# Quantised W1 rows of a four-layer residual kernel: turned through memory and VectorE instead of TensorE, and five of the seven threshold steps nested between VectorE and ScalarE

## The reference, cut to what matters

```
def _L1_cond_ref(x, weight, scale_log, codebook, lora_A, lora_B):
    lora_delta = lora_B @ lora_A * (32.0 / 64)
    cb = codebook / clip(max(abs(codebook)), 1e-08)          # 8 levels
    scale = exp(scale_log)                                    # one for each row and group of 128
    normalized = (weight + lora_delta).reshape(O, I // 128, 128) / scale
    thresholds = (cb[:-1] + cb[1:]) * 0.5                     # 7 thresholds
    idx = searchsorted(thresholds, normalized, side='left')
    quantized = cb[idx]
    w_q = quantized * scale
    return x @ (w_q + lora_delta).T

x = x + _L0_cond_ref(...)    # W0, with a low-rank part chosen by batch
x = x + _L1_cond_ref(...)    # W1, as above
x = x + _L2_cond_ref(...)    # W2, with a low-rank part chosen by batch
x = x + _L3_cond_ref(...)    # W3, with a router and eight small experts
```

## Time and profile before

| | |
|---|---|
| median of 3 runs (lowest to highest) | 594.34 us (594.05 to 594.41) |
| span of the profiled execution | 592.8 us |
| PE busy | 585.1 us, 99% |
| DVE busy | 447.3 us, 75% |
| ACT busy | 236.4 us, 40% |
| POOL busy | 111.9 us, 19% |
| granted TensorE clock | 1.000 |

### The profile page before, as it was taken

One profiled execution on the slowest core, in us unless ns is written; L12 is line 12 of the kernel. 1 busy time (PEld: TensorE's weight loads), 2 busy tenths in 40 slices (PEclk: granted clock), 3 DMA queues, 4 the chain that ended last, 5 costly groups with the idle time before them and its releaser, 6 DMA issues.

```text
span 592.8 us, 9183 instructions
## 1 busy us (share of the span) xinstructions
PE 585.1 (99%) x3152; PEld 522.2 (88%) x3152; DVE 447.3 (75%) x812; ACT 236.4 (40%) x482; POOL 111.9 (19%) x131
## 2 busy tenths in 40 slices
PE   7999999999999999999999999999999999999998
PEld 6999999899999999999787887787888888888887
DVE  4678998999989855897788999947474747474744
ACT  4534233445432216544465477323333333333331
POOL 3101010012000000336324011041212121212110
PEclk9999999999999999999999999999999999999999
DMA  8962230173000000000243000223031303131301
GB/s 258 231 173 79 87 110 2 26 187 125 1 2 1 1 0 2 2 0 2 25 87 77 1 1 1 65 79 105 37 101 41 107 34 102 40 94 48 107 1 71
DMA packets 56994, 37.19 MB, mean 63 GB/s; under 512 B 25924, under 2 KB 50756, under 8 KB 56964
## 3 DMA queue, kind: packets, MB, share of 16 engines
q1 hardware_dynamic: 56964, 36.79, 22.2%
HBM read 28.39 MB, written 8.39 MB: 62 GB/s over the span
## 4 chain that ended last, share of the span: by engine, by line
PE 73%; DVE 22%; issue 2%; ACT 1%; SPq 1%; DMA 1%; POOL 0%; DVEq 0%; ACTq 0%
PE acc L1864 39%; PE acc L1718 16%; DVE q L1244 6%; PE aux L1864 5%; DVE qtmp L1243 4%; PE acc L1985 4%; PE aux L1706 2%; PE acc L1987 2%; DVE hg_lo L1270 1%; PE acc L1993 1%; PE acc L1994 1%; DVE w_lo L1131 1%; DVE a_t L1255 1%; DMA g<-in_L_cond_W_dram 1%; DVE a_t L1246 1%
## 5 line engine op out<-in xcount | busy, mean ns | idle before, releaser
L1864 PE MATMUL acc<-b_hi,g_lo 128*128 128x512 f32 (+1 forms) x266 | 88.9, 389 | 0.1
L1864 PE MATMUL acc<-t_hi,g_lo 128*128 128x512 f32 x256 | 87.6, 400 | 0.0
L1718 PE MATMUL acc<-hg_hi,w_hi 128*128 128x352 f32 (+1 forms) x376 | 85.3, 334 | 1.6 <-DVE hg_lo L1270 0.8
L1718 PE MATMUL acc<-hg_lo,w_hi 128*128 128x352 f32 (+1 forms) x376 | 84.3, 331 | 0.0
L1718 PE MATMUL acc<-hg_hi,w_lo 128*128 128x352 f32 (+1 forms) x376 | 84.0, 330 | 0.0
L624 POOL TENSOR_TENSOR xr<-xr 128x512 f32<-128x512 f32 x32 | 41.1, 1308 | 144.3 <-DVE g_lo L1435 142.9
L1718 PEld LDWEIGHTS acc<-hg_hi,w_hi 128*128 128x128 f32 x376 | 65.1, 188 | 3.0 <-DVE hg_lo L1270 1.1
L1718 PEld LDWEIGHTS acc<-hg_hi,w_lo 128*128 128x128 f32 x376 | 65.8, 188 | 0.0
L1718 PEld LDWEIGHTS acc<-hg_lo,w_hi 128*128 128x128 f32 x376 | 65.8, 188 | 0.0
L1244 DVE TENSOR_TENSOR q<-q,qtmp 128x1024 f32<-128x1024 f32 x48 | 59.7, 1243 | 1.7
L1864 PEld LDWEIGHTS acc<-b_hi,g_lo 128*128 128x128 f32 x266 | 49.6, 188 | 11.2 <-DVE part L1606 0.5
(11 more groups left out here) (301 smaller groups left out, 1140.2 us busy)
## 6 DMA issues: line engine op xcount, KB each, us to landing
out_dram<-part SPq DMA_DIRECT2D x31, 256.0 KB, 2.8
x_st<-in_x_dram SPq DMA_DIRECT2D x60, 128.0 KB, 2.9
g<-in_L_cond_W_dram SPq DMA_DIRECT2D x8, 512.0 KB, 6.3
a_t<-in_L_cond_weight_dram SPq DMA_DIRECT2D x8, 512.0 KB, 5.6
w_raw<-in_L_cond_weight_dram SPq DMA_DIRECT2D x8, 512.0 KB, 4.0
w_st<-in_L_cond_W_dram SPq DMA_DIRECT2D x7, 512.0 KB, 4.0
a_raw<-in_L_cond_lora_A_dram SPq DMA_DIRECT2D x5, 128.0 KB, 3.5
a_raw<-in_L_cond_lora_A_dram SPq DMA_DIRECT2D x20, 32.0 KB, 1.9
```

The costliest lines, as they stand in the source:

```text
L1718: last = pe.matmul(acc[0:a.shape[-1], slot, bank * BANK:bank * BANK + c1 - c0], a[:, k, :], b[:, k, c0:c1], start=(at == 0 and n == 0), st ...
L1864: last = pe.matmul(dst, p, q, start=start and n == 0, stop=stop and n == 2, skip_group_check=True)
```

## The change

1. **Turning.** A finished tile goes from `a_t` to a DRAM tensor `w1_rows` in four transfers of 32 partitions each (128 KB), and comes back in one of 512 KB into `wq`, so that the four 32-row quarters lie where a DVE transpose, which turns 32x32 blocks, makes the whole 128x128 turn of them: two STREAM_TRANSPOSE of 128x512 into `wt`. `wq` and `wt` lie in the room of `w_st`. `w1_high` and `w1_low` read `wt`. The 64 transposes on PE go. SP issues 40 transfers more in its one queue, `rows_back(1)` ahead of the loads of W0.
2. **Nesting.** The thresholds 6, 5, 4, 3, 2 are nested: DVE makes q = (n > threshold) * q in one SCALAR_TENSOR_TENSOR, ACT then adds the next step to q, in halves of 512 columns, by turns. The thresholds 1 and 0 stay plain; the last plain one also adds the lowest level. The finish is 8 SCALAR_TENSOR_TENSOR of 128x128, q * scale + ldelta.
3. **Order.** `delta(5)`, `delta(6)`, `delta(7)` move ahead of passes 6, 7, 9; `w2_low`, `copy_delta` and `out_g` stand at other places between the threshold steps; `a2_raw` moves to the room of `a_hi`, and is loaded after the last `delta`.

```diff
+    NEST = (6, 5, 4, 3)
-        a2_raw = place("a2_raw", 154368, [P, KT, LABELS * R])
+        wq, wt = place("wq", 154368, [P, D]), place("wt", 158464, [P, KT, P])
+        a2_raw = place("a2_raw", 121600, [P, KT, LABELS * R])
...
+            def rows_away(n):
+                sp.wait_ge(w1e_done, n + 1)
+                for c in range(QUARTERS):
+                    sp.dma_start(w1_rows[n].rearrange("(a r) (c f) -> c r a f", r=Q, c=QUARTERS)[c],
+                                 row(n, slice(c * Q, (c + 1) * Q)).rearrange("r (a f) -> r a f", a=QUARTERS)
+                                 ).then_inc(rows_out[n], 16)
+            def rows_back(n):
+                sp.wait_ge(rows_out[n], 16 * QUARTERS)
+                if n == 0:
+                    sp.wait_ge(w_split, splits(KT - 2))
+                else:
+                    sp.wait_ge(w1_t, 2 * n)
+                sp.dma_start(wq[:], w1_rows[n]).then_inc(wq_in, 16)
+            rows_away(0)
+            rows_back(0)
+            rows_away(1)
+            rows_away(2)
+            rows_away(3)
+            rows_back(1)
             for k in range(KT):
                 wait_used(sp, KT, k)
                 sp.dma_start(w0_raw[:, k, 0:D], W0[k * P:(k + 1) * P, :]).then_inc(w0_in[k], 16)
                 sp.dma_start(w0_raw[:, k, D:C_A], B0[k * P:(k + 1) * P, :]).then_inc(w0_in[k], 16)
+            rows_away(4)
+            rows_back(2)
...
+            def raise_(n, j):
+                for h in range(2):
+                    ks = slice(h * HALF, (h + 1) * HALF)
+                    act.wait_ge(dq_step, 2 * (n * len(NEST) + NEST.index(j)) + h + 1)
+                    act.add(q[:, ks], q[:, ks], steps[:, j - 1:j]).then_inc(dq_added, 1)
...
-            def quantise(x, part, steps_=None):
...
+            def nest(x, *js):
+                for j in js:
+                    for h in range(2):
+                        ks = slice(h * HALF, (h + 1) * HALF)
+                        n = a_t[:, x, 0:D].rearrange("p (k i) -> p k i", k=KT)[:, ks]
+                        if j == NEST[0]:
...
+                            dve.tensor_scalar(q[:, ks], n, th(j), steps[:, j:j + 1], ALU.is_gt, ALU.mult).then_inc(dq_step, 1)
+                            continue
+                        dve.wait_ge(dq_added, 2 * (x * len(NEST) + NEST.index(j + 1)) + h + 1)
+                        step = dve.scalar_tensor_tensor(out=q[:, ks], in0=n, scalar=th(j), in1=q[:, ks],
+                                                        op0=ALU.is_gt, op1=ALU.mult)
...
+            def plain(x, j):
+                link(dve.tensor_scalar(qtmp[:], n, th(j), steps[:, j:j + 1], ALU.is_gt, ALU.mult))
+                if j:
+                    link(dve.tensor_tensor(q[:], q[:], qtmp[:], ALU.add))
+                else:
+                    link(dve.scalar_tensor_tensor(out=q[:], in0=qtmp[:], scalar=book[:, 0:1], in1=q[:],
+                                                  op0=ALU.add, op1=ALU.add))
+            def finish_w1(x):
+                for k in range(KT):
+                    last = dve.scalar_tensor_tensor(
+                        out=at[:, k], in0=q[:, k].rearrange("p (a q) -> p a q", a=QUARTERS), scalar=scale[:, x, k:k + 1],
+                        in1=ldelta[x % 2][:, k * P:(k + 1) * P].rearrange("p (a q) -> p a q", a=QUARTERS),
+                        op0=ALU.mult, op1=ALU.add)
+            def turn_w1(n):
+                dve.wait_ge(w_split, splits(KT + n - 1))
+                dve.wait_ge(wq_in, 16 * (n + 1))
+                for half in range(2):
+                    ks = slice(half * HALF, (half + 1) * HALF)
                    dve.transpose(wt[:].rearrange("p k (c r) -> p c k r", r=Q)[:, :, ks].bitcast(U32),
                                  wq[:].rearrange("p (c k q) -> p c k q", c=QUARTERS, q=Q)[:, :, ks].bitcast(U32)
                                  ).then_inc(w1_t, 1)
...
-            def turn_w1(n):
-                pe.wait_ge(w1e_done, n + 1)
...
-            DELTA_FIRST = {3: 2, 4: 3, 5: 4, 7: 5}
-            DELTA_AT = {(1, 3): 0, (1, 6): 1, (10, 0): 6, (12, 0): 7}
+            DELTA_FIRST = {3: 2, 4: 3, 5: 4, 6: 5, 7: 6, 9: 7}
+            DELTA_AT = {(1, 3): 0, (1, 6): 1}
```

More of the change, by code:

```diff
@@ L359, in build @@
         n_ready = sem("n_ready")
+        dq_step, dq_added = sem("dq_step"), sem("dq_added")
         w1e_done = sem("w1e_done")
+        rows_out, wq_in = [sem(f"rows_out{n}") for n in range(KT)], sem("wq_in")
         w1_t = sem("w1_t")
@@ L505, in _ @@
                 sp.dma_start(w0_raw[:, k, D:C_A], B0[k * P:(k + 1) * P, :]).then_inc(w0_in[k], 16)
+            rows_away(4)
+            rows_back(2)
+            rows_away(5)
+            rows_back(3)
+            rows_back(4)
+            rows_away(6)
+            rows_back(5)
+            sp.wait_ge(ld_done, KT)
+            for l in range(LABELS):
+                sp.dma_start(a2_raw[:, :, l * R:(l + 1) * R], A2[l].rearrange("(k p) r -> p k r", p=P)).then_inc(a2_in, 16)
+            rows_away(7)
+            rows_back(6)
+            rows_back(7)
             def load_x(row, dst=x_st, landed=x_in):
@@ L795, in _ @@
+            raise_(3, 4)
+            raise_(3, 3)
             copy_delta(4)
+            normalise(4)
             w2_step(7)
             out_g(5)
+            for j in NEST:
+                raise_(4, j)
+            copy_delta(5)
             out_g(6)
-            normalise(4)
-            copy_delta(5)
+            normalise(5)
+            w1_high(0)
             act.wait_ge(acc_done, B2_PASS + 1)
             evacuate(bp[R:2 * R, :], B2_PASS % 2, 0, R, C_LOW2)
-            w1_high(0)
-            for k in range(6):
+            raise_(5, 6)
@@ L806, in _ @@
+            raise_(5, 5)
+            copy_delta(6)
+            raise_(5, 4)
+            w0_high(0)
+            raise_(5, 3)
+            for k in range(1, 5):
                 w0_high(k)
-            out_g(7)
-            for k in range(6, KT):
+            normalise(6)
+            for k in range(5, KT):
                 w0_high(k)
             w1_high(1)
-            normalise(5)
-            out_a(0)
-            copy_delta(6)
-            w1_high(2)
+            out_g(7)
+            raise_(6, 6)
@@ L1234, in split_b2 @@
                                          op0=ALU.mult, op1=ALU.subtract).then_inc(b2_done, 1)
[L1236 to L1250 removed]
+            def nest(x, *js):
[4 more added lines that the diff above has]
+                        if j == NEST[0]:
+                            dve.wait_ge(n_ready, G1 * x + HALF * (h + 1))
+                            if x:
+                                dve.wait_ge(w1e_done, x)
+                            dve.tensor_scalar(q[:, ks], n, th(j), steps[:, j:j + 1], ALU.is_gt, ALU.mult).then_inc(dq_step, 1)
[3 more added lines that the diff above has]
+                                                        op0=ALU.is_gt, op1=ALU.mult)
+                        if j in NEST:
+                            step.then_inc(dq_step, 1)
+                        else:
+                            link(step)
```

178 lines of the change are left out of this document (108 added, 70 removed).

## The result

The changed kernel takes 610.06 us (median; 608.99 to 610.20), the kernel before 594.32 in the same session: ratio 1.0267, 95% interval 1.0253 to 1.0282, slower. 608.5 was forecast, range 598 to 618. The span of the profiled execution grew from 592.8 to 608.3 us.

A forecast was written before the change was run, and what follows sets the result against it. PE was taken as the bound, DVE narrowly behind. Late dates 12.2, less 0.9 for an extra delta, plus 5.4 and 4.5, minus 7.0 saved: +14.2 on span 592.8, 607.0; median 608.5, range 598 to 618.

The forecast's parts named there:

- Prices: Durations assumed per new DVE or ACT instruction, such as 0.71 us an addition and 0.75 a nested half step.
- Finishes: End times of W1 tiles 0 to 3 on DVE, from going through the queues in written order; period 17.8 us.
- Dates: PE's pass starts, missed because copies of delta stand behind ACT's additions: 12.2 us late by pass 7.
- Pass 9: W0's splits interleaved with tile 5's nested steps: PE waits four times, 6.2 us together, in place of 0.8.
- Low parts: Passes 10, 13 and 14 wait for w1_low on DVE: 1.6, 2.3 and 0.6 us.
- PE's saving: PE no longer turns eight tiles of W1, 0.87 us each: 7.0 us, all on the path.
- The way: Tiles' trip through memory, near 10 us, costed at nothing because DVE's own lateness hides it.
- L1853: Source line given, in the signs of being right, for PE idling before it to wait for DVE's hg_lo.
- DVE has 3 us a period less to do: DVE's own work per tile period falls from 18.1 to 15.1 us before handovers; cited in favour of the faster rival.
- handovers and detours: DVE waiting for ACT's additions, 0.8 us a tile, and for ACT's other jobs standing between them, 1.9.
- Faster: Rival: handovers cost nothing (addition with handovers under 0.59 us) and detours hide, giving 586.5 us; chance 0.12.

The follow-up runs named there:

- one_transpose: The kernel before with one 128x128 transpose per tile of W1 on PE instead of eight: 590.46 us, ratio 0.9943.
- new_order: All the changed kernel's instructions, with DVE, ACT and SP queues reordered and PE's deltas of tiles 5, 6, 7 at their old places: 587.36 us, ratio 0.9888.
- the three single repairs: The changed kernel with, separately, copies of delta earlier on ACT (613.04 us), two PE deltas one pass later (609.19), W0's splits ahead of tile 5's later steps (612.5).
- splits_low_first: The changed kernel with W0's splits and tile 1's low part ahead of tile 5's steps from threshold 4 on, on DVE and ACT: 612.5 us.
- tiny_additions: The changed kernel with ACT's 64 additions cut to 8 columns each, all waits and queue places kept: 598.12 us, ratio 1.0071 to the kernel before.
- deltas_later: The changed kernel with PE's deltas of tiles 5 and 6 one pass later, ahead of passes 7 and 8: 609.19 us.
- short_way: The changed kernel with wq filled straight from input W1, not waiting for the rows sent to memory; outward transfers still run: 609.64 us.
- memory_plain: The kernel before with the turn through memory and on DVE, all seven thresholds on DVE, queues ordered anew: 595.71 us, ratio 1.003.

## Why the prediction was right

By its own steps, forecast and then measured:

- *Prices.* Addition 0.71: 0.721. Nested half step 0.75: 0.761. First threshold half 0.55: 0.540. Finish 0.35: 0.347. Turn 688 ns: 692. Only the plain addition was off, 1.25 against 1313 ns: five of its eight took 1.36 to 1.37 us.
- *Finishes* of tiles 0 to 3 ending at 63.9, 81.7, 99.4, 115.6: at 63.3, 81.3, 99.3, 115.7. The period was 18.0 twice, then 16.4; 17.8, 17.7 and 16.2 had been forecast. That is partly luck: in the first two, DVE waited 2.0 us for additions, where 0.8 + 1.9 had been put, and its own work with the gaps between instructions took 16.0, where 15.1 had been put. Before 124 us these waits come to 5.6 us, where some 7 had been forecast.
- *Dates.* PE's deltas behind the copies, forecast for 72.9, 90.7, 107.9, 124.1: 72.33, 90.33, 107.88, 124.28. At pass 7 PE was 12.4 us late (124.28 less 111.87), 12.2 forecast.
- *Pass 9.* Four waits, 6.2 forecast: from start to start 5.9 (their idle time is 4.8; each also costs the overlap of two matmuls and a slower first one, some 0.25). In the same count the one wait of before is 1.1. So 4.8 in place of 5.4.
- *Low parts*, 1.6, 2.3 and 0.6 forecast ahead of passes 10, 13 and 14, 4.5 in all: 3.7 idle, 4.5 in the same count, but ahead of passes 10, 12 and 13.
- *PE's saving*, 7.0: supported by one_transpose and new_order. *The way*, nothing: three runs. The row to look for is L1851; "L1853" in the prediction's last part was a slip.

12.4 - 0.9 + 4.8 + 4.5 - 7.0 is 13.8; the passes ended 15.5 us late. The missing 1.7 are a term that the prediction does not have: after two of its waits PE ran at half its clock. Windows of 2 us, PE's busy time (count), clock, DMA share, GB/s:

```profile
90.00:92.00 2.00, 1.67 (x5) 0.65 0.00 0
92.00:94.00 2.00, 2.00 (x8) 0.50 0.65 190
94.00:96.00 2.00, 2.00 (x13) 0.99 1.01 235
...
125.00:127.00 2.00, 2.00 (x7) 0.50 0.20 43
127.00:129.00 2.00, 2.00 (x10) 0.71 0.56 219
129.00:131.00 2.00, 2.00 (x13) 1.00 0.00 0
```

0.50 is 1.2 GHz, 1.00 the full 2.4. From 124.28 to 128.97 PE did a delta and four rows of three matmuls, which take 0.91 + 4 x 0.53 us at full clock (112.78 less 111.87 and 113.31 less 112.78 in the kernel before): 1.7 us lost ahead of pass 9, on the path. The first fall cost as much, but in front of the wait at 107.88 for ACT, where the time would have been spent waiting. This is arithmetic on the trace; no run took the clock's fall away by itself.

What the prediction had less right is its reading of the sum. It lists a price for each date missed, as if each could be bought back; the three single repairs gave 0.9 less, 2.4 more and 3.0 more. And it took "DVE has 3 us a period less to do" for spent on handovers and detours, where the new order, with the same waits on DVE, is faster than both kernels. Its rival *Faster* had two conditions, additions under 0.59 and detours that hide. The first does not decide: with additions of 0.30 the change is still slower than before, with 0.72 in the new order it is faster. The second does, and the prediction took the written order for given.

## What to carry to other kernels

With two engines near saturation, price what an edit frees on one against what it puts on the next: here one half cost 1.4 us alone, the other won 1.3, both together won 6.9. When the order of a stage is written by hand, new instructions need a new order: first what a waiting engine wants, long chains behind it, and no item finished earlier than its reader needs (these three are what the new order does here; none was run alone). A wait that can be removed by a local edit is not a cost until a run shows that the next wait does not take its place. And before a difference of 1 us is given a cause, the traces should show that it arises in the stretch that was edited.

## What was not expected of the hardware

- The clock fell to 0.50 after a wait of 3.71 us and, for some 3 us of the trace, after one of 2.51; not after 2.07 at 107.88 or 2.10 at 193.33. In splits_low_first the same wait before pass 7, 2.52 us, left it at 1.00, and so did one of 2.83. After 2.13 in tiny_additions, 2.14 in deltas_later and 1.93 in short_way it was at 0.50. The length of the wait alone did not tell, in these runs. The falls in the changed kernel cost 1.7 us each beyond the wait itself, the one in tiny_additions 1.6.
- In memory_plain the 7.5 us wait is followed by such a stretch too, which cost some 1.9 us (the first five rows of pass 9 took 4.36 us, from 141.42 to 145.78, where 5 x 0.48 is the spacing of full clock):

```profile
141.00:143.00 2.00, 1.58 (x5) 0.50 0.00 0
143.00:145.00 2.00, 2.00 (x8) 0.50 0.00 0
145.00:147.00 2.00, 2.00 (x13) 0.87 0.00 0
```

- The plain addition (L1334) took 1.36 to 1.37 us five times (at 75.50, for one) and 1.22 to 1.23 three times (at 181.85, for one). All five long ones, and all six of 1.36 or 1.37 us among the 48 additions of the kernel before, overlap an instruction of POOL, which adds the unit matrix in SBUF; no addition without one is long. ACT's normalising, which runs beside most of them too, does not tell them apart: beside ACT alone, for its whole length, an addition of the kernel before took 1.23 (at 99.04). DVE and POOL of the changed kernel, a long one and what stood beside it:

```profile
156.14 1.37 DVE L1334 TENSOR_TENSOR q<-q,qtmp 128x1024 f32<-128x1024 f32 x1
```

```profile
155.51 0.91 POOL L618 TENSOR_TENSOR ldelta<-ldelta,ident 128x128 f32<-128x128 f32 x1
```

  Two additions of the kernel before that overlap POOL's work on W0 stayed at 1.22, and no run took POOL's instruction away, so this is an observation and not a cause shown.
